# A selective-scan kernel: four stages of the first layer rewritten, and scan step 24 fed through TensorE

## What is computed

```python
tn = (t - mu) * rsqrt(var + 1e-05) * ln_g + ln_b      # t: windows x 64 positions x 128 channels
xi, z = split(tn @ W_in + b_in)                        # 2 x 256 channels
xc = silu(causal_conv4(xi) + conv_b)
dr, Bm, Cm = split(xc @ W_x)                           # 8, 16 and 16 columns
delta = softplus(dr @ dt_w + dt_b);  A = -exp(A_log)
for each position:                                     # h: windows x 256 x 16 states
    h = exp(delta * A) * h + (delta * xc) * B_t;  y = sum_over_states(h * C_t)
y = (y + xc * D) * silu(z)
x1 = y @ W_out + b_out + x
```

## Time and profile before

| | us |
|---|---|
| median of three runs | 9233.19 |
| these runs | 9228.69 to 9234.46 |
| the profiled execution, its own time | 9233.49 |
| its span (first to last instruction) | 9231.7 |

### The profile page before, as it was taken

How to read it: one execution, slowest core, us unless ns; L and a number is a source line. 1 busy time by engine, 2 the same in 40 slices (tenths; PEclk the granted TensorE clock), 3 DMA queues, 4 the chain that set the end, 5 groups by cost and what they waited for, 6 DMA issues and landing times. The chain is left out here.

```text
span 9231.7 us, 162156 instructions
## 1 busy us (share of the span) xinstructions
PE 8609.1 (93%) x54525; PEld 6725.1 (73%) x54525; DVE 8294.6 (90%) x8144; ACT 7704.9 (83%) x13926; POOL 8062.4 (87%) x3865
## 2 busy tenths in 40 slices
PE   7999999999999999999999999999799999999999
PEld 4666666666666666666666666666689999999788
DVE  5999999999999999999999999999889999999766
ACT  6999999999999999999999999999755555555577
POOL 5999999999999999999999999999789999999500
PEclk9999999999999999999999999999999999999999
DMA  3333333333333333333333333333311111110255
GB/s 92 109 120 111 118 110 120 113 116 111 121 113 115 112 120 115 113 113 119 117 110 114 120 115 110 114 122 113 100 39 34 37 36 34 37 37 33 90 185 181
DMA packets 648481, 931.99 MB, mean 101 GB/s; under 512 B 79960, under 2 KB 277600, under 8 KB 643552
## 3 DMA queue, kind: packets, MB, share of 16 engines
q1 hardware_dynamic: 647904, 924.64, 31.8%
HBM read 778.38 MB, written 146.04 MB: 100 GB/s over the span
## 5 line engine op out<-in xcount | busy, mean ns | idle before, releaser
L1035 POOL TENSOR_TENSOR prod<-state,c_all 128x1024 f32<-128x1024 f32 x1280 | 3028.2, 2371 | 72.6 <-DVE state L909 72.6
L1024 POOL TENSOR_TENSOR drive_d<-du,b_all 128x1024 f32<-128x1024 f32 x1024 | 2424.3, 2368 | 13.7 <-issue 12.4
L909 DVE TENSOR_TENSOR_SCAN state<-decay_d,drive_d 128x1024 f32<-128x1024 f32 x1024 | 2336.9, 2282 | 77.1 <-ACT decay_d L724 77.0
L909 DVE TENSOR_TENSOR_SCAN state<-decay_r,drive_r 128x1024 f32<-128x1024 f32 x1024 | 2323.4, 2269 | 27.9 <-PE drive_r L581 16.1
L594 PEld LDWEIGHTS y_acc<-ident,prod 128*128 128x128 f32 x16384 | 1867.2, 142 | 630.8 <-issue 524.3
L594 PE MATMUL y_acc<-ident,prod 128*128 128x128 f32 x16384 | 2160.0, 276 | 42.4 <-POOL prod L1035 38.5
L1332 DVE SCALAR_TENSOR_TENSOR sum_d<-bank_d,filt,sum_d 128x512 f32<-128x512 f32 x2470 | 1654.2, 742 | 119.2 <-PE bank_d L1240 119.2
L737 ACT ACTIVATE ub<-ut,bt 128x256 f32<-128x256 f32 x4096 | 1739.1, 500 | 12.4 <-PE drive_r L581 12.0
L1379 POOL TENSOR_TENSOR sum_p<-sum_p,scaled 128x1024 f32<-128x1024 f32 x650 | 1555.1, 2392 | 79.0 <-ACT scaled L1290 31.3
L1290 ACT ACTIVATE scaled<-bank_p,filt 128x512 f32<-128x512 f32 x1560 | 945.5, 689 | 621.6 <-PE bank_p L1240 613.3
L724 ACT ACTIVATE decay_d<-delta,neg_a 128x504 f32<-128x504 f32 x2048 | 1312.0, 674 | 79.8 <-DVE state L909 78.7
(11 more groups left out here) (155 smaller groups left out, 14646.3 us busy)
## 6 DMA issues: line engine op xcount, KB each, us to landing
c_all<-bc_rows SPq DMA_DIRECT2D x1280, 256.0 KB, 3.3
b_all<-bc_rows SPq DMA_DIRECT2D x1024, 256.0 KB, 3.8
ys<-row_spectra SPq DMA_DIRECT2D x130, 256.0 KB, 2.8
column_sums<-tt SPq DMA_DIRECT2D x130, 256.0 KB, 2.1
x_in<-in_x_dram SPq DMA_DIRECT2D x64, 512.0 KB, 4.9
x_res<-in_x_dram SPq DMA_DIRECT2D x64, 512.0 KB, 5.0
x_rows<-x SPq DMA_DIRECT2D x64, 512.0 KB, 4.5
row_spectra<-z SPq DMA_DIRECT2D x64, 512.0 KB, 3.7
```

Source lines behind the costliest of these rows:

```text
L909: dve.tensor_tensor_scan(state[n % NT][:].rearrange("p h t -> p (h t)"), decay[:].rearrange("p h w t -> p (h w t)"), drive[:].rearrange("p ...
L1024: pool.tensor_tensor(drive_d[place_of(DSTEPS, n, ND)][:], du[:, :, q * HT:(q + 1) * HT], b_all[slot][:].unsqueeze(1).to_broadcast([P, 2, HT]),
L1035: pool.tensor_tensor(prod[n % NP][:], state[n % NT][:], c_all[slot][:].unsqueeze(1).to_broadcast([P, 2, HT]), ALU.mult).then_inc(s["prod_g ...
```

## The change

1. **Layer norm.** `mean_w` is replaced by `centre_w = ident - mean_w` in the `mean` job, so that PSUM holds x minus its mean at once. ACT squares it from PSUM; DVE multiplies it by the reciprocal deviation into a tile `tn` of its own (`normalise`, in place of `centre`). GpSimd's `make_tn` goes.
2. **delta.** The bias dt_b becomes one more row of `dt_w` (against a row of ones). ACT takes |v| alone; DVE makes delta = max(v, 0) + soft in one instruction (`take_dt`, two per half). GpSimd's `add_soft` goes.
3. **xc * D.** `add_skip` goes; each `turn` job starts with one matmul of `diag_d` with 512 columns of xc, and the transposes of y are added onto it.
4. **ut and bt.** Three of four `ut` copies go from DVE to ACT; the `bt` jobs use four transposes for four matmuls.
5. **Step 24** goes from `DSTEPS` to `RSTEPS`: PE turns its drive, and GpSimd scales `ut` by B in four pieces of 128x256 at half step 42 (`UB_AT`).
6. **Products.** GpSimd has 23 of 32 (new: 4, 14, 24 and 26; gone: 20), DVE nine: 0, 2, 6, 10, 16, 20, 22, 28, 30.
7. The tables `JOBS` and `AT` are new throughout, ring places run on over blocks, and `pick` has 16 columns read by a broadcast.

```diff
-DSTEPS = tuple(n for n in range(NSTEP) if n % 2 == 0)
-RSTEPS = tuple(n for n in range(NSTEP) if n % 2 == 1)
+DSTEPS = (0, 2, 4, 6, 8, 10, 12, 14, 16, 18, 20, 22, 26, 28, 30)
+RSTEPS = tuple(n for n in range(NSTEP) if n not in DSTEPS)
+UB_AT = {24: 42}
-BY_GPSIMD = tuple(sorted(RSTEPS + (8, 12, 18, 20)))
+BY_GPSIMD = (1, 3, 4, 5, 7, 8, 9, 11, 12, 13, 14, 15, 17, 18, 19, 21, 23, 24, 25, 26, 27, 29, 31)
...
-    (12, "conv10", "front", 1), (15, "turn11", "back", 0), (18, "z01", "front", 0), (18, "conv01", "front", 1),
+    (15, "conv10", "front", 1), (16, "z01", "front", 0), (18, "ut01", "scan", 0), (20, "bt1", "scan", 0),
+    (20, "z11", "front", 1), (22, "conv01", "front", 1), (23, "ut11", "scan", 0), (25, "conv11", "front", 0),
...
             def turn_drive(step):
                 M, p, n = step
                 scanned(pe, *before_in(RSTEPS, M, n, 1))
-                need(pe, s["ub_done"], upto(RSTEPS, M, n))
+                if n in UB_AT:
+                    need(pe, s["ub_g_done"], upto(scaled_by(True), M, n))
+                else:
+                    need(pe, s["ub_done"], upto(scaled_by(False), M, n))
...
-            def add_skip(p, q, g):
-
-                for k in range(2):
-                    pe.matmul(y_acc[:, g, k * P:(k + 1) * P], xc[p][:, k, q * HT + g * P:q * HT + (g + 1) * P],
-                              wt["diag_d"][:, k, :], start=False, stop=False, skip_group_check=True)
...
-                    M = m if q == 0 else m - 1
+                    M, par = (m, p) if q == 0 else (m - 1, f)
+                    pe.matmul(misc[:], wt["diag_d"][:, hf, :], xc[par][:, hf, q * HT:(q + 1) * HT], start=True,
+                              stop=False, skip_group_check=True)
...
-                    if n + 1 in RSTEPS and S.scan:
+                    if n + 1 in RSTEPS and n not in RSTEPS and S.scan:
                         turn_drive(S.step(n + 1, p))
...
+                    if n + 1 in RSTEPS and n in RSTEPS and S.scan:
+                        turn_drive(S.step(n + 1, p))
...
             def softplus(S, M, q):
 
-                taken(act, S, f"dt0{q}", f"dt1{q}")
-                n = M * 4 + 2 * q
+                for hf in range(2):
+                    misc = full(act, S, f"dt{hf}{q}")
+                    act.activation(soft[:, hf, :], misc[:], ACT.Abs).then_inc(s["softplus_done"], 1)
...
+            def take_dt(S, hf, q):
+                M = S.m + 1 if q == 0 else S.m
+                misc = full(dve, S, f"dt{hf}{q}")
+                need(dve, s["softplus_done"], M * 8 + 4 * q + 4)
...
+                dve.scalar_tensor_tensor(delta[:, hf, q * HT:(q + 1) * HT], misc[:], 0.0, soft[:, hf, :], ALU.max,
+                                         ALU.add).then_inc(take(S, f"dt{hf}{q}"), 1)
...
-            def add_soft(M, q, hf):
-                need(pool, s["softplus_done"], M * 4 + 2 * q + 2)
-                d = delta[:, hf, q * HT:(q + 1) * HT]
-                pool.tensor_tensor(d, d, soft[:, hf, :], ALU.add).then_inc(s["delta_done"], 1)
-
-            def make_du(M, q, hf, p):
-
-                need(pool, s["delta_done"], (M * 2 + q) * 2 + hf + 1)
+            def scale_u(S, step):
+                M, p, n = step
+                q, st = n // NS, n % NS
+                need(pool, s["drive_r_done"], upto(RSTEPS, *before_in(RSTEPS, M, n, NS_UB)))
...
+                for g in range(4):
+                    last = pool.tensor_scalar(ub[place_of(RSTEPS, M, n, NS_UB)][:, g, :], ut[q][:, g, :],
+                                             bt[q][:, g, st:st + 1], None, ALU.mult)
+                last.then_inc(s["ub_g_done"], 1)
+
+            def make_du(S, M, q, hf, p):
+                taken(pool, S, f"dt{hf}{q}")
...
```

234 lines of the change are left out of this document (128 added, 106 removed), and 22 rows, old and new, of tables (AT, JOBS).

## The result

The changed kernel takes 9285.69 us (median of 4 runs, 9282.18 to 9290.52), the kernel before 9231.79 beside it: ratio 1.0059, 95% interval 1.0046 to 1.0071. Forecast were 9105 us, with 9260 as the upper end of the range, and "slower" had 0.16. The direction was wrong, and the time was missed by 181 us, 2.8 us in each of 64 blocks.

The account below looks back on a forecast made before the run. Prediction: the block costs its fullest engine (GpSimd, 96.77 us) plus some 5.4 us of mutual waiting. The walk cut 102.41 us a block to 100.4, 64 x 2.0 = 128 us less, giving 9105 us; range 8970 to 9260.

Parts of the forecast that it names:

- my walk: Order followed through one block from the turning of step 9's drive: 99.6 us by rows, 100.4 us with handovers.
- Scan 15: Steps 9 to 15: PE's longer list delays scan 15 to 21.0 us from 19.07, losing 1.9 us.
- Scan 25: Steps 21 to 25: DVE stands 1.1 to 1.2 us for step 24's turned drive.
- DVE's wait ahead of the first `take_dt`: Steps 15 to 20: GpSimd's wait for softplus moves to DVE, shrinking from 2.71 to between 0 and 0.9 us.
- Rival 2: `take_dt` puts DVE's scans behind ACT's softplus: 103.4 us a block, 9297 us; chance 0.13.
- handovers: Gaps of 0.1 us or so, eight to ten on the block's path, raising 99.6 us to 100.4.
- The work of the engines: Busy time per block: GpSimd 95.4 to 96.7 us, DVE 92.8, ACT 96.0 to 96.1 (fullest), PE 93.2.
- the signs: Wrong if: period outside 99 to 101.8 us, DVE's ln waits over 2, no scan 15 wait, piece above 0.73, clock below 1.00.
- Steps 25 to 8: Block's last part: from scan 31 PE has 25.7 us, DVE 23.9 plus 0.4 and 0.6; both end at 99.1 to 100.0.
- My rival for the clock: More transposes pull PE's granted clock down, PE needing about 186 us a block: 14600 us; chance 0.01.
- The Trainium skill's rule: Transposes don't count as busy the way matmuls do, so the change would move PE towards the lower clock; no size given.
- a piece of `ub`: GpSimd's scaling of `ut` by B for step 24: 0.40 us a piece taken, 0.73 the upper bound.

Follow-up runs that it names:

- the early bank: Changed kernel with relu left out of delta and ACT's |v| freeing the dt banks: 9375.11 us; its control, banks still freed by `take_dt`, 9451.47 us.

## Why the prediction was wrong, step by step

**Right.** Most of what lies ahead of the failed step, counted as in my walk (t = 0 at the turning of step 9's drive), in DVE's timeline of the changed kernel:

```profile
3155.44 2.29 DVE L922 TENSOR_TENSOR_SCAN state<-decay_r,drive_r 128x1024 f32<-128x1024 f32 x1 [3.17 <-ACT decay_r L737]
...
3190.39 2.29 DVE L922 TENSOR_TENSOR_SCAN state<-decay_r,drive_r 128x1024 f32<-128x1024 f32 x1 [1.24 <-issue]
...
3209.71 2.28 DVE L922 TENSOR_TENSOR_SCAN state<-decay_d,drive_d 128x1024 f32<-128x1024 f32 x1
```

- Scan 15 stands 21.07 us behind the turning of 9 (3134.37); the walk said 21.0. DVE waits 3.17 there, said about 3. The profile names ACT's decay as the releaser, but that had long been done; PE's turning of 15 began at 3154.31.
- Scan 25 waits 1.24 us (said 1.1 to 1.2); step 24 costs 0.94 us a block by the run that takes it back.
- GpSimd no longer waits for ln, and DVE's wait ahead of the first `take_dt` is 0.35 us (said 0 to 0.9). Rival 2, softplus in front of DVE, is not what happened, though its time (9297) is the one nearest to the result.
- From scan 15 to scan 0 of the next block 54.27 us; the walk said 53.5, and I had added 0.8 for handovers. That it fits is luck: the dip behind `mean0` lies in this stretch, and the six blocks without it take 53.1 to 53.2 (2844.75 to 2897.89 us in the one shown above).
- The work of the engines: DVE 92.9 (said 92.8), ACT 96.1 (96.0 to 96.1), PE 94.0 (93.2). GpSimd has 97.6 (95.4 to 96.7), by the price of the pieces.

Three of the signs that I had named for being wrong came up: a period of 103.25 us, a piece above 0.73 us and a clock below 1.00 in the block.

**The step that failed** is the last of the walk, "Steps 25 to 8". It let PE run its 25.7 us of work from scan 31 to the turning of 9 beside DVE's 23.9, as two chains of which the longer one counts. Scan 0 at 3209.71 to the turning of 9 at 3237.11 is 27.40 us; the walk had about 25.1. They are no two chains: PE must stop at `turn11` for DVE's `take_dt` of half 1, since both banks hold v until then, and only after it does the list of 4.56 us begin that leads to the turning of 9, and the 19.94 from there to that of 15. DVE's stretch and PE's lie in series, and DVE in its turn then stands 1.1 to 1.3 us for `turn11` ahead of the gate. I had read from the diff that `take_dt` reads v from PSUM, and had priced its instruction; that it also takes over from ACT's relu the freeing of the bank, three instructions of softplus later, I did not follow to PE. This stretch is 2.3 us too short in the walk, and so is the whole of an ordinary block (102.70 us over the forecast's 100.4), 147 us in all.

Two engines are late at this point within half a microsecond of each other, which the wait's one name hides. ACT's ln of half 1 and DVE's `take_dt`, in the block of 3232.55:

```profile
3230.42 1.06 ACT L791 ACTIVATE soft<-soft 128x1024 f32<-128x1024 f32 x1
...
3231.84 1.26 DVE L973 SCALAR_TENSOR_TENSOR delta<-job_bank,soft 128x512 f32<-128x512 f32 x2
```

The ln ended at 3231.48 and `take_dt` began 0.36 us later, behind scan 7. Putting `take_dt` ahead of that scan would therefore free the bank at most 0.4 us sooner, an estimate from these two rows; no run tried it.

**The clock** is the second term: I had 1.00 through the block and the trace has 0.98. The dips behind `turn11` are 35 us and those behind `mean0` some 70, 1.6 us a block together. The second of these is inside the 102.70 us of the ordinary block and doesn't show in the sum, since the 0.8 us for handovers and a stretch counted 0.3 us too long made up for it. Without any dip the changed kernel's block would be 101.6 us, an estimate from its stretches without one (18.7 us from the table load to `mean0`, 55.6 to `turn11`, 27.3 to the next load): 1.2 us over the forecast are then left for the waits themselves, beside 1.6 for the clock behind them. My rival for the clock was built on a share of transposes; that is not what decides here. From the turning of 9 to that of 15 PE ran mostly such records at 1.00, and in the 60 blocks it fell to 0.50 only behind the two new waits. The Trainium skill's rule ("TensorE: Matmul & The Clock Gate", Part 4), weighed in the prediction, would have put the loss in the stretches full of transposes; the trace does not show it there. (147 and 35 add up to the 181 us that were missed because both come from the mean of the same 60 blocks; the sum proves nothing.)

**Mis-sized but without effect**: a piece of `ub` at 0.925 us, where 0.40 was taken and 0.73 was the upper bound. The bound was drawn from a multiply with two tensor inputs, and the form with one number per partition was dearer than that, not cheaper. A saving of 1.8 us there moved nothing. The wait of GpSimd for a load of B behind the store of yo was not in the walk either, and moving the store gained nothing.

**Shown and open.** Shown: step 24's price; that GpSimd's work and the late load, each alone, are off the path; that time put into DVE before `take_dt` of half 1 comes back at one to one and time put into PE between there and the turning of 15 at more, while at PE's end of the block 1.7 us cost 1.2; that the early bank gives 1.2 us a block in a control whose `take_dt` was slower than the real one; and what the two dips cost. Only argued: how the rest divides between the hold and DVE's and ACT's being late there in the real form of `take_dt`. No run freed the bank with nothing else changed. That the dips follow from the waits is read from their place, behind the two waits and nowhere else in 60 blocks; a PE kept busy through the wait wasn't tried.

## What to carry to other kernels

When an edit moves the reader of a PSUM bank, ask who frees the bank now and when, and write that instruction into the walk of the engine that writes the bank: with two banks and two long holders, two chains that ran side by side can become one. Then read the granted clock behind each new wait of PE: here the dips made more than half of the miss. An engine that is the fullest by busy time need not set the pace (GpSimd, busy for 4725 of 5000 us, gave back 1.8 us for nothing); put a microsecond in, or take one out, before spending effort there. And the cheapest gain was not in the order at all, but in making the chain itself shorter: one ACT instruction and two DVE instructions less per half gave 3.1 us of a block.

## What the runs showed of the hardware that I had not expected

- A DVE instruction of 128x1024 took 2.27 us with one input in PSUM and 3.44 at the median with both in SBUF, ending 2.15 us after GpSimd's running instruction. With one input, in SBUF alone, 128x512 took 0.43 us or waited for GpSimd just so (a pair in 3.80 us for 0.76). Moving decay_d out of its two PSUM banks cost 1562 us.
- GpSimd's multiply by one number per partition took 0.925 us for 128x256; the same work as one multiply of 128x1024 with a broadcast took 1.905, half of the four.
- After PE had waited 2.14 us the granted clock fell to 0.50 in 21 of 60 blocks, and after 2.65 us in 54 of 60; a dip cost 1.6 us of a block behind the first wait and 1.2 behind the second. The waits and the order of instructions are the same in blocks with and without a dip.
